# Spreading eight product additions over GpSimd, VectorE and TensorE, with a third raw image and nine product buffers

## What is computed

```python
x = x + L0(gn(x))                       # adaptive 3x3 aggregation
x = x + conv3x3(conv3x3(conv3x3(gn(x), w1), w2), w3)
```

## Time and profile before

| what | us |
|---|---|
| median of three runs | 593.44 |
| the profiled execution | 597.1 |
| its span, first to last instruction | 595.2 |
| TensorE busy in it | 496.5 |
| VectorE busy | 431.7 |
| GpSimd busy | 277.7 |
| ScalarE busy | 149.2 |
| mean granted clock of TensorE | 0.866 |

### The profile page before, as it was taken

One profiled execution on the slowest core, in us unless ns is written; L12 is line 12 of the kernel. 1 busy time (PEld: TensorE's weight loads), 2 busy tenths in 40 slices (PEclk: granted clock), 3 DMA queues, 4 the chain that ended last, 5 costly groups with the idle time before them and its releaser, 6 DMA issues. The chain is left out here.

```text
span 595.2 us, 8487 instructions
## 1 busy us (share of the span) xinstructions
PE 496.5 (83%) x3484; PEld 291.5 (49%) x3484; DVE 431.7 (73%) x483; ACT 149.2 (25%) x247; POOL 277.7 (47%) x104
## 2 busy tenths in 40 slices
PE   1999995975796877984696969796989897999996
PEld 1998893864342433552252534353344633454443
DVE  3135989999579979999579989968599989941000
ACT  1326151223520140131620051033312151022000
POOL 0410362678026843978027754856049643960000
PEclk9996586986599878998598869988979697998999
DMA  5000000103120000103330010121202100310301
GB/s 136 5 0 5 1 2 0 36 1 81 51 67 1 1 20 18 36 3 78 80 73 2 1 35 1 36 53 29 72 20 61 29 8 1 79 36 16 90 10 36
DMA packets 27926, 19.49 MB, mean 33 GB/s; under 512 B 22064, under 2 KB 22640, under 8 KB 27888
## 3 DMA queue, kind: packets, MB, share of 16 engines
q1 hardware_dynamic: 27888, 18.95, 13.1%
HBM read 5.16 MB, written 4.19 MB: 16 GB/s over the span
## 5 line engine op out<-in xcount | busy, mean ns | idle before, releaser
L1864 POOL TENSOR_TENSOR prod<-prod 128x2048 f32<-128x2048 f32 x43 | 195.4, 4549 | 122.3 <-DVE prod L1063 96.3
L428 PE MATMUL conv_ps<-xq,kb 128*64 128x512 f32 x768 | 201.9, 661 | 0.0
L1063 DVE TENSOR_TENSOR prod<-val_ps,tapw 128x2048 f32<-128x2048 f32 x80 | 181.2, 2280 | 15.5 <-PE val_ps L481 14.8
L428 PEld LDWEIGHTS conv_ps<-xq,kb 128*64 128x64 f32 x768 | 54.7, 146 | 92.9 <-issue 92.6
L498 PE MATMUL agg_ps<-ident_sb,prod 128*128 128x128 f32 x480 | 75.2, 317 | 21.1 <-ACT agg L1640 16.8
L498 PEld LDWEIGHTS agg_ps<-ident_sb,prod 128*128 128x128 f32 x480 | 65.6, 166 | 38.0 <-ACT agg L1640 20.5
L1880 POOL TENSOR_TENSOR xs<-xn 128x1024 f32<-128x1024 f32 x32 | 69.7, 2195 | 28.1 <-PE val_ps L481 18.9
L481 PE MATMUL val_ps<-ident_sb,xs 128*128 128x128 f32 x256 | 48.4, 320 | 27.4 <-DVE prod L1063 25.9
L1640 ACT ACTIVATE agg<-agg_ps 128x512 f32<-128x512 f32 x64 | 36.6, 594 | 120.5 <-PE agg_ps L498 120.3
L481 PEld LDWEIGHTS val_ps<-ident_sb,xs 128*128 128x128 f32 x256 | 33.2, 163 | 57.5 <-DVE prod L1063 42.8
L1854 POOL TENSOR_TENSOR gn<-gn,powers 128x2 f32<-128x2 f32 x8 | 7.7, 959 | 60.2 <-DVE gn L897 60.2
(11 more groups left out here) (116 smaller groups left out, 545.7 us busy)
## 6 DMA issues: line engine op xcount, KB each, us to landing
xq<-y SPq DMA_DIRECT2D x128, 70.0 KB, 2.0
xraw<-in_x SPq DMA_DIRECT2D x32, 128.0 KB, 2.8
out_y<-outb SPq DMA_DIRECT2D x32, 128.0 KB, 2.8
xn<-xn SPq DMA_DIRECT2D x16, 24.8 KB, 1.9
w_in<-in_w SPq DMA_DIRECT2D x1, 384.0 KB, 3.2
w_in<-in_w SPq DMA_DIRECT2D x1, 192.0 KB, 4.6
w_sb<-in_w SPq DMA_DIRECT2D x1, 96.0 KB, 3.2
sel_sb<-in_sel_quarter SPq DMA_DIRECT2D x1, 64.0 KB, 2.6
```

The lines of the kernel that those rows point to most:

```text
L428: mm = nc.tensor.matmul(bank[part, :], w, src[:, every, cols], start=n == 0, stop=False)
L1063: v.tensor_tensor(dst, val.unsqueeze(2).to_broadcast([P, B, R, C]), wgt.unsqueeze(3).to_broadcast([P, B, R, C]), ALU.mult).then_inc(mult_d ...
L1864: p.tensor_tensor(product(i, TAPS * h + a), product(i, TAPS * h + a), product(i, TAPS * h + b), ALU.add).then_inc(add_g, 1)
```

## The change

The table of additions, the buffers and the lists of all engines are changed; the helpers stay the same except for the waits that follow from the buffers. In image 0 GpSimd made one addition of each half, in image 1 five, in images 2 to 7 six of eight; now it makes none in image 0 and two in each other one. VectorE makes two in image 0 and three in the others, TensorE the rest. The ten units have nine product buffers (units 1 and 9 share one), the raw image has three. The load and the store of an image are one transfer each. Room for the buffers comes from aliases: the raw weights lie where the output tiles are later, the value weights in `x2`, the half-made 7x7 kernel in the second buffer of `xq`, so that `by_slots` of image 1 waits for the finished kernel. A helper for adds by DMA is there, but no entry of the table uses it.

```diff
-N_AGG, N_CONV = 2, 2
+N_AGG, N_CONV, N_X = 2, 2, 3
-SUMS = [('GTTT', 'GTTT'), ('GGGT', 'GGVT'), ('GGGT', 'GGVG'), ...
+SUMS = [('VTTT', 'VTTT'), ('GVTT', 'GVVT'), ('GVTT', 'GVVT'), ...
-UNIT_BUF = (0, 1, 2, 3, 1, 4, 5, 6, 3, 5)
-N_PROD = 7
+UNIT_BUF = (0, 1, 2, 3, 4, 5, 6, 7, 8, 1)
+N_PROD = 9
...
-                if j >= 2:
-                    wait(x2_done, 2 * (j - 2) + 2)
-                for g in range(G):
-                    sp.dma_start(xraw[C * g:C * g + C, j % 2, :],
-                                 x[j, :, QR * g:QR * g + QR, :].rearrange("c r w -> c (r w)")).then_inc(x_in[j % 2], 16)
+                if j >= N_X:
+                    wait(x2_done, 2 * (j - N_X) + 2)
+                src = x[j, :, :, :].rearrange("c (g r) w -> g c (r w)", g=G)
+                sp.dma_start(xraw[:, j % N_X, :], src).then_inc(x_in[j % N_X], 16)
...
-                for s in range(4):
-                    dst = out[j, :, :, :].rearrange("c (q s) w -> c q s w", s=4)[:, :, s, :]
-                    sp.dma_start(dst, outb[C * s:C * s + C, j % 2, :, :]).then_inc(out_st[j % 2], 16)
+                dst = out[j, :, :, :].rearrange("c (q s) w -> s c q w", s=4)
+                sp.dma_start(dst, outb[:, j % 2, :, :]).then_inc(out_st[j % 2], 16)
...
-                if u % TAPS == 1 and i >= 1:
-                    wait_consumed(dve, i - 1, h, 3)
+                if u == 1 and i >= 1:
+                    wait_consumed(dve, i - 1, 1, 3)
+                if u == 6 and i >= 1:
+                    wait_consumed(dve, i - 1, 1, 0)
...
-                if u == 3 and i >= 1:
-                    wait_consumed(dve, i - 1, 1, 1)
-                if u == 8:
-                    wait_consumed(dve, i, 0, 1)
-                if u % TAPS == 4:
-                    wait_consumed(dve, i, h, 0)
+                if u % TAPS == 3 and i >= 1:
+                    wait_consumed(dve, i - 1, h, 1)
+                if u == 4 and i >= 1:
+                    wait_consumed(dve, i - 1, 0, 3)
+                if u == 9:
+                    wait_consumed(dve, i, 0, 0)
```

More of the change, by code:

```diff
@@ L159, in conv_l0_l1_kernel @@
         pads_p = sem("pads_p")
-        x_in = [sem(f"x_in_{n}") for n in range(2)]
+        x_in = [sem(f"x_in_{n}") for n in range(N_X)]
         gn1_v = sem("gn1_v")
@@ L176, in conv_l0_l1_kernel @@
         add_g = sem("add_g")
+        add_d = [[sem(f"add_d_{h}_{n}") for n in range(4)] for h in range(2)]
         agg_t = sem("agg_t")
@@ L207, in wait_added @@
                 eng.wait_ge(add_g, adds_by("G", i, h, n + 1))
+            elif SUMS[i][h][n] == "D":
+                eng.wait_ge(add_d[h][n], 16 * sum(SUMS[m][h][n] == "D" for m in range(i + 1)))
         def wait_consumed(eng, i, h, n):
@@ L582, in _ @@
             values(0, 8)
-            second_weights(3, 0)
             transpose_sums(0, 3)
             values(0, 9)
-            second_weights(3, 1)
+            second_weights(4, 1)
+            pointwise(0, 0)
+            geometry(2)
             values(1, 0)
-            pointwise(0, 0)
+            second_weights(5, 0)
+            values(1, 1)
             transpose_sums(0, 4)
-            values(1, 1)
             transpose_sums(0, 5)
@@ L652, in _ @@
+            values(2, 7)
+            values(2, 8)
+            convs(0, 40, 41)
+            pointwise(2, 0)
+            convs(0, 41, 50)
+            values(2, 9)
+            convs(0, 50, 60)
             values(3, 0)
-            transpose_sums(2, 2)
-            convs(0, 43, 49)
-            transpose_sums(2, 3)
-            convs(0, 49, 54)
             values(3, 1)
-            convs(0, 54, 60)
-            convs(1, 0, 1)
-            pointwise(2, 0)
-            convs(1, 1, 13)
-            values(3, 2)
@@ L668, in _ @@
+            pointwise(2, 1)
             values(3, 3)
-            convs(1, 14, 18)
-            pointwise(2, 1)
+            convs(1, 12, 15)
             values(3, 4)
-            convs(1, 18, 21)
+            convs(1, 15, 28)
             values(3, 5)
-            convs(1, 21, 31)
+            convs(1, 28, 31)
+            gn2_sums(2, 0)
+            convs(1, 31, 34)
+            gn2_sums(2, 1)
             values(3, 6)
-            convs(1, 31, 33)
-            values(3, 7)
-            convs(1, 33, 35)
@@ L690, in _ @@
-            convs(1, 38, 41)
-            gn2_sums(2, 1)
-            convs(1, 41, 42)
-            geometry(4)
-            pointwise(3, 0)
-            convs(1, 42, 44)
+            values(3, 9)
+            convs(1, 38, 54)
             values(4, 0)
-            convs(1, 44, 51)
+            convs(1, 54, 55)
             values(4, 1)
-            convs(1, 51, 60)
+            convs(1, 55, 60)
+            convs(2, 0, 2)
             transpose_sums(3, 4)
             transpose_sums(3, 5)
+            gn1_sums(5, 1)
@@ L728, in _ @@
-            convs(2, 43, 44)
+            convs(2, 36, 38)
             transpose_sums(4, 0)
             transpose_sums(4, 1)
-            convs(2, 44, 49)
+            values(4, 7)
+            convs(2, 38, 39)
+            transpose_sums(4, 2)
+            values(4, 8)
+            transpose_sums(4, 3)
+            convs(2, 39, 40)
+            values(4, 9)
+            pointwise(4, 0)
+            convs(2, 40, 41)
             values(5, 0)
-            convs(2, 49, 60)
-            convs(3, 0, 1)
+            convs(2, 41, 42)
@@ L747, in _ @@
+            pointwise(4, 1)
+            geometry(6)
+            convs(3, 10, 11)
+            gn2_sums(4, 0)
+            convs(3, 11, 13)
+            gn2_sums(4, 1)
+            convs(3, 13, 32)
+            gn1_sums(7, 0)
+            convs(3, 32, 34)
+            values(5, 2)
+            convs(3, 34, 36)
             values(5, 3)
-            convs(3, 12, 13)
-            pointwise(4, 1)
+            convs(3, 36, 39)
             values(5, 4)
-            convs(3, 13, 15)
+            convs(3, 39, 41)
@@ L1865, in add_products, with add_by_dma @@
                                 ALU.add).then_inc(add_g, 1)
+            def add_by_dma(i, h, n):
+                if SUMS[i][h][n] != "D":
+                    return
+                a, b = ADDS[n]
+                pool.wait_ge(mult_done, UNITS * i + TAPS * h + max(a, b) + 1)
+                for m in range(n):
+                    wait_added(pool, i, h, m)
+                p.dma_start(product(i, TAPS * h + a), product(i, TAPS * h + b),
+                            accum_op=ALU.add).then_inc(add_d[h][n], 16)
             def pair_sum(i, n):
```

868 lines of the change are left out of this document (416 added, 452 removed).

## The result

The changed kernel takes 540.77 us (median of four runs, 538.98 to 543.87) beside 593.64 for the kernel before on the same chip: ratio 0.911, 95% interval 0.905 to 0.916. It is 52.9 us faster, where 34 were forecast. The profiled execution took 540.62 us with a span of 538.7, which is 56.5 less than before. Two of the four executions of experiment e2 and one of the four of e6 (its profiled one) were slower than the others of the same kernel, so the times and ratios given for e2 and e6 leave them out; with it e6 has the 520.1 us that one expectation names.

The account below looks back on a forecast made before the run. No engine was full; the end followed VectorE's last instruction, so VectorE's time for eight images was counted. Terms -58.9 + 36.6 - 22.0 + 11.1 - 1.35 = -34.6 took 597.1 to 562.5 us, 559 as a median; range 524 to 600.

Parts of the forecast that it names:

- A: GpSimd adds: 29 of 43 go, each freeing 2.03 us of VectorE's time, -58.9 us.
- B: VectorE's additions: 16 adds come to it at the median of 2.285 us each, +36.6 us.
- C: VectorE's waits for geometry, ScalarE and the pointwise product shrink as images are prepared earlier, -22.0 us.
- D: TensorE gets 13 more additions, 208 transposes, of which +11.1 us shows in the time.
- E: Loads and stores: one load transfer lets the weights behind it be issued sooner, -1.35 us; the single store counted 0.
- rival 3: GpSimd adds: the 14 left run beside multiplications only, another 28.4 us go, median 530.8; chance 0.20.
- rival 2: VectorE's 16 new adds are each held by 2.2 us, +34.7, so no change, median 593.6; chance 0.07.
- Geometry: VectorE's waits for a coming image's first normalisation and its geometry, 9.2 us, all go.
- Pointwise: VectorE's 18.8 us of waits for the pointwise product: 10.7 stay, half of the other 8.1 goes, -4.0 us.
- The waits for ScalarE: VectorE's 17.6 us of waits inside the tap weights halve, -8.8 us, as these spread over every image's multiplications.
- Rival 1: TensorE becomes the bound, its gaps stay and the 208 transposes add in full, median 617.5; chance 0.16.
- the prediction's check: TensorE between the cuts: 434.5 us of work at the present clocks in 453.7 us would be 96% busy.

Follow-up runs that it names:

- e2: The changed kernel with only the stores in four transfers again, loads still in one: 536.8 us, ratio 0.903 to the kernel before.
- e6: e1 with the first image's chain back in the order of the kernel before: 518.1 us, ratio 0.872 to the kernel before.
- e3: The kernel before with the new table of additions, nothing else moved: 574.1 us, ratio 0.967 to the kernel before.
- e11: e1 with eleven parts of the tap weights moved back between the products of second halves: 536.0 us, ratio 0.901 to the kernel before.
- e12: e6 with three small VectorE instructions moved, two behind products and one ahead of a product: 514.1 us, ratio 0.868 to the kernel before.
- e10: e1 with the old table of additions for images 1 to 7, 41 adds on GpSimd: 582.7 us, ratio 0.980 to the kernel before.
- e7: The kernel before with a third raw image alone: 594.1 us, ratio 0.999 to the kernel before.
- e1: The changed kernel with loads and stores in four transfers again: 522.0 us, ratio 0.878 to the kernel before.
- e5: e1 with seven additions moved from TensorE to VectorE, 112 transposes fewer: 533.6 us, ratio 0.897 to the kernel before.

## Why the prediction was right, and where its sizes were off

The mechanism held: GpSimd's adds hold VectorE's small instructions, and the end follows VectorE's last instruction at 49 to 53 us. The sum is off by 22 us. By its terms, on the span:

| term | forecast | measured | from |
|---|---|---|---|
| A, stalls beside adds | -58.9 | -73.3 | 87.3 to 14.0 |
| stalls beside pair sums | 0 | -20.6 | 28.8 to 8.2 |
| B, 16 adds on VectorE | +36.6 | +36.5 | 16 x 2.28 |
| rest of VectorE's busy time | 0 | -5.4 | 413.5 to 350.6 less the above, not traced further |
| VectorE's idle time (C, and D's shares) | -10.9 | -6.6 | 74.8 to 68.2 |
| before the first product (E) | -1.35 | +9.3 | 58.0 to 67.3 |
| behind VectorE's last | 0 | +3.6 | 48.9 to 52.5 |
| sum | -34.6 | -56.5 | |

**A was under-sized.** "I take the mean, since the 14 are of the same size and stand among the same neighbours": the size is the same, the neighbours are not. With the old neighbours (e3) an add that stays costs 1.66 us instead of 2.03, in the new lists 1.0. In the new lists the small instructions of the tap weights stand more behind the products than between them; e11 put eleven back and lost 14.0 us, e12 moved three more and halved the excess of adds and pair sums together. So a part of rival 3 took place, which forecast 28.4 more on the adds; 14.4 came.

**The pair sums were counted as unchanged.** They were not in the sum at all, though the prediction had counted their 28.8 us. The table alone does not lower them (36.1 in e3), nor do the orders alone to this extent (24.5 in e10); both together do (8.2).

**B was right.** 22 of 23 adds run undisturbed; rival 2, in which the lock only changes hands, needed most of them held. Now and then it does change hands, to the other side: a pair sum that starts behind a VectorE add is held by it, first VectorE and then GpSimd:

```profile
363.37 2.28 DVE L1070 TENSOR_TENSOR prod<-prod 128x2048 f32<-128x2048 f32 x1
```

```profile
364.73 2.79 POOL L1903 TENSOR_TENSOR xs<-xn 128x1024 f32<-128x1024 f32 x1 [2.01 <-PE val_ps L486]
```

The pair sum's median is 2.01 us, and another, at 90.84, takes 3.67. No run shows that this costs time; GpSimd is busy 27% of the span.

**C was right in two of three places and lost elsewhere.** Geometry: -9.2 forecast; 9.2 fell to 0.3, though another wait for a sum of the statistics grew from 1.8 to 5.7. Pointwise: -4.0 forecast, 18.8 fell to 14.1. The waits for ScalarE were to halve; in the same three places 17.6 fell to 14.4, and 5.8 came at another line (1004). The loads brought 11.3 us of new waits for the raw image. The second multiplication of an image, which I feared would queue behind transposes, waits 0.7 us in all. The prediction put the earlier loads down to the third raw image; by itself it brings nothing (e7), it only makes the new lists possible.

**D was not a cost that can be seen.** The clock and the filling of gaps paid for it: busy time between the cuts fell from 408.9 to 387.0 us, with the clock at 0.94 where it was 0.85. Rival 1, TensorE as the bound, needed its idle share to stay at 17%; from 155 to 445 us it fell from 17.9% (238.2 of 290 busy, row at the end) to 4.3%. That VectorE is still waited for where TensorE is 97% busy (e1) is shown by e5, in which work taken off TensorE and given to VectorE cost 11.7 us. One reading of the gaps before was off: between 160 and 500 us TensorE waited 25.6 us for VectorE's products, as the prediction says, but directly for GpSimd's adds only 0.5; 15.9 were waits for ScalarE's copies of the sums. What the 208 transposes cost by themselves was not measured.

**E had the wrong sign.** "The first load takes SP 1.79 us in four issues, so the weights behind it are issued 3 x 0.45 = 1.35 us sooner": they were issued sooner (the raw weights at 5.33 us instead of 6.36) and landed later, for the transposes at 15.41 instead of 12.06. TensorE began at 14.34, not near 10.7, and the last store took twice as long. "All other loads and stores are issued tens of microseconds before their data are needed" failed too: the loads of images 2 to 7 already began only 5 to 7 us ahead of their statistics in the kernel before, those of images 3 to 7 begin 8 to 26 us ahead now, and VectorE waits 11.3 us in three places for a raw image (in e1 2.4 in one). I counted issues and not what one transfer can move. Going back to four transfers gives 18.8 us (e1). At the store the prediction did ask whether issuing and moving would still overlap, but allowed 2 us for it; 5.2 were lost. Of the 9.3 us ahead of the first product 2.7 go with the single transfer; the other 6.6 come with the new lists and are not explained further.

That the time lies in the range is partly luck, since two errors met: the new lists took away 35 us of stalls that the sum had not counted (14.4 beside adds, 20.6 beside pair sums), and the single transfers cost 18.8. Without that loss the time would have been 522, below the range's lower end of 524.

## What to carry to other kernels

A stall between two engines is priced by its neighbours, not by its count: before the mean stall is carried over, list which instruction will stand beside each one in the new order, and put PSUM-fed work there. A table that says who does what, and the order in which it is done, are one change: here each alone gave 10 to 20 us and both together 72. And "one transfer instead of four" saves issue time only; look at the share of DMA engines and the GB/s of such a transfer first.

## What of the hardware was not expected

**One transfer of 512 KB was slower here than four of 128 KB.** The single store shows a DMA share of 0.25 to 0.32 at 47 to 73 GB/s, the four of e1 show 0.63 to 1.08 at 101 to 214 GB/s (windows of 1 us while they run; the view's share can come out above 1). The Trainium skill (DMA: Bandwidth & Descriptors, "Rules for kernel authors") says that a transfer whose outermost dimension is smaller than 16 is confined to that many engines; here that dimension is 4, and 4 of 16 are 0.25. The trace agrees, nearly: 0.32 is the most it shows. Had the prediction used that rule, E would have pointed the other way.

**More forms are held by a GpSimd add than "reads SBUF twice".** A TENSOR_SCALAR with one tile of input was held (407.40 in e11: 4.45 us, median 0.22), as was the prediction's own first example at 182.73. Nor does a small size help: a SCALAR_TENSOR_TENSOR on 128 x 1 was held (385.21: 4.45 us, 0.22), while a TENSOR_SCALAR on 128 x 1 passed (187.10: 0.20 us, the add running since 186.92). The Trainium skill (SBUF — State Buffer, "Who interferes with whom") says that issue order decides who blocks; the two rows at 385 agree, the add having started 0.09 us earlier. Its section on the two sides of SBUF ("SBUF: two separate sides") names, beside two inputs, VectorE's modes that use two ports; whether the TENSOR_SCALAR ran in one, no run here shows.

**The clock followed the filling.** The same window of the kernel before:

```profile
155.00:445.00 290.00, 238.22 (x1628) 116.83 (x1628) 248.41 (x270) 71.30 (x116) 155.93 (x51) 0.86 0.14 35
```

The granted clock there is 0.86 with TensorE busy 238.2 us; it is 0.96 with 277.5 in the changed kernel, 0.97 with 280.9 in e1 and 0.99 with 284.4 in e12. So the 208 transposes more were done in less busy time (387.0 us between the cuts) than the mix of clocks before would have needed (434.5 by the prediction's check).
